# Expert tile rows turned by VectorE from four feature groups, gates spread by a block transpose

## What is computed

```
def _L0_ffn_ref(x, gate_w, gate_b, w1, b1, w2, b2, w3, b3):
    K = 2
    logits = jnp.einsum('bsd,de->bse', x, gate_w) + gate_b
    probs = jax.nn.softmax(logits, axis=1)
    vals, idx = jax.lax.top_k(probs, K)
    h = relu(einsum('bsd,edo->ebso', x, w1) + b1[:, None, None, :])
    h = relu(einsum('ebso,eop->ebsp', h, w2) + b2[:, None, None, :])
    y = relu(einsum('ebso,eop->ebsp', h, w3) + b3[:, None, None, :])
    onehot = one_hot(idx, E)
    w_tok = einsum('bske,bsk->bse', onehot, vals)
    v = einsum('ebso,bse->eo', y, w_tok)
    return einsum('bse,eo->bso', onehot.max(axis=2), v)
```

## Time and profile before

| | us |
|---|---|
| median of 3 runs (1003.84, 1006.84, 1004.35) | 1004.35 |
| span of the profiled execution | 1003.7 |
| expert stage in it, PE's first transpose to the end of the last unit | 437.9 to 669.6 |

### The profile page before, as it was taken

The page is one execution under the profiler, slowest core; times in us unless marked ns, Lnnn a source line. Parts: engine busy times, 40 slices in busy tenths (PEclk is TensorE's granted clock), DMA queues, the critical chain, the costliest instruction groups (busy, mean ns, idle before and its releaser), DMA issues. The chain is left out here.

```text
span 1003.7 us, 19227 instructions
## 1 busy us (share of the span) xinstructions
PE 934.0 (93%) x7747; PEld 757.2 (75%) x7747; DVE 429.3 (43%) x994; ACT 346.5 (35%) x886; POOL 250.9 (25%) x306
## 2 busy tenths in 40 slices
PE   5999999989998889999999999999889899999994
PEld 5977776676775644789999999987765578999532
DVE  2973454224442647002112132135267630656576
ACT  2322323245552124122222233324276611122374
POOL 5452111023554306000000010004065403000275
PEclk9999999999999979899999999997969998999996
DMA  9994000245622807259999888700040032971001
GB/s 254 382 331 127 2 2 2 98 152 203 238 120 95 309 7 254 55 181 386 358 383 313 284 269 283 254 29 28 4 153 3 2 119 78 321 247 66 1 15 51
DMA packets 72456, 162.01 MB, mean 161 GB/s; under 512 B 4132, under 2 KB 5685, under 8 KB 70321
## 3 DMA queue, kind: packets, MB, share of 16 engines
q1 hardware_dynamic: 70048, 156.54, 45.8%
q0 software_dynamic: 2320, 4.25, 1.4%
HBM read 128.81 MB, written 31.97 MB: 160 GB/s over the span
## 5 line engine op out<-in xcount | busy, mean ns | idle before, releaser
L2113 PE MATMUL ps<-ffn_h,ffn_w 128*128 128x128 f32 x1280 | 149.1, 275 | 0.0
L2113 PEld LDWEIGHTS ps<-ffn_h,ffn_w 128*128 128x128 f32 x1280 | 145.9, 192 | 0.0
L2113 PE MATMUL ps<-ffn_xh,ffn_w 128*128 128x128 f32 x640 | 74.9, 275 | 0.3 <-ACT ffn_xh L2147 0.3
L2203 DVE TENSOR_SCALAR ffn_h<-ps,tile_bias 128x128 f32<-128x128 f32 x80 | 22.5, 345 | 122.4 <-PE ps L2113 122.4
L2113 PEld LDWEIGHTS ps<-ffn_xh,ffn_w 128*128 128x128 f32 x640 | 73.1, 192 | 0.9 <-issue 0.9
L1418 POOL TENSOR_TENSOR ctx_low<-shelf,ctx_high 128x1024 fp32r<-128x1024 f32 (+2 forms) x24 | 43.0, 1819 | 65.4 <-PE ps L1283 33.7
L2161 ACT ACTIVATE ffn_y<-ffn_y 128x128 f32<-128x128 f32 x80 | 23.7, 298 | 73.9 <-DVE ffn_y L2219 73.9
L1526 PE MATMUL ps<-x_qT,ctx_ct 128*128 128x100 f32 (+1 forms) x384 | 46.4, 284 | 2.3 <-PEq L137 2.0
L1526 PEld LDWEIGHTS ps<-x_qT,ctx_ct 128*128 128x128 f32 (+1 forms) x384 | 45.0, 197 | 3.7 <-issue 3.2
L2219 DVE SCALAR_TENSOR_TENSOR ffn_y<-ps,tile_bias,ffn_gate_row 128x128 f32<-128x128 f32 x80 | 22.6, 344 | 58.0 <-PE ps L2113 57.9
L2834 POOL TENSOR_TENSOR att_e<-att_e,decay 100x400 f32<-100x400 f32 x32 | 32.7, 1033 | 46.1 <-DVE att_e L2685 46.1
(11 more groups left out here) (469 smaller groups left out, 2096.8 us busy)
## 6 DMA issues: line engine op xcount, KB each, us to landing
ffn_w<-in_L_ffn_w_dram SPq DMA_DIRECT2D x60, 1024.0 KB, 6.0
shelf<-in_ctx_dram SPq DMA_DIRECT2D x12, 1280.0 KB
expert_rows<-nothing SPq DMA_DIRECT2D x1, 14820.0 KB, 49.6
context_turned<-ctx_ct SPq DMA_DIRECT2D x8, 1444.0 KB, 7.9
ctx_ct<-context_turned SPq DMA_DIRECT2D x8, 1444.0 KB, 12.5
ctx_lent<-in_ctx_dram SPq DMA_DIRECT2D x4, 1280.0 KB
rows_own<-expert_rows SPq DMA_DIRECT2D x8, 260.0 KB, 3.0
x_wo<-in_L_xattn_Wo_dram SPq DMA_DIRECT2D x1, 2048.0 KB, 9.5
```

The lines of the kernel that those rows point to most:

```text
L2113: mm = nc.tensor.matmul(acc(n)[:, m, :], w[:, n % SLOTS, k, m * P:(m + 1) * P], into[l][:, i % 2, k, :], start=k == 0, stop=k == C - 1, sk ...
L2203: nc.vector.tensor_scalar(h2[:, i % 2, m, :], acc(n)[:, m, :], bsel[:, m, i, 1:2], 0.0, ALU.add, ALU.max).then_inc(h2_kept, 1)
```

## The change

**Loading the rows.** The one DMA of a tile becomes eight. For each block n of 32 rows, one DMA loads the 512 features as four groups of 128: the group f of the block's row r goes to partition 32 f + r, columns 128 n to 128 n + 127. A second DMA loads the 8 gates of these 32 rows onto each of the four groups of 32 partitions, into the new buffer `gates_raw`, with a semaphore of its own.

**Turning them.** DVE's transpose turns each 32x32 block in place of it. With the rows laid out in four groups, one such instruction of 128x512 gives `xh` directly: partition 32 f + d' of column (n, k, r) is feature 128 f + 32 k + d' of row 32 n + r. PE's transposes and ACT's copies are gone. A product k of the first layer now sums over the features 128 f + 32 k + d' instead of 128 k + p, so the first layer's weights must have their rows in that order: `load_unit` loads l = 0 as four DMAs of 256 KB, one for each k, whose source walks 4 groups x 32 rows x 2 KB. Its right-hand side is four pieces of 32 columns. The other two layers are loaded as before.

**Gates.** POOL and DVE work on four columns of gates at once; a second DVE transpose, of the broadcast 128x4 gates, puts them on all partitions. PE's product and ACT's copy are gone.

**Order.** The 14 later gathers stand behind every second unit load (odd n, 5 to 31) instead of behind each; the six `last` loads follow at n = 32 to 37.

The diff, cut to its core:

```diff
+        first_w = g["L0_ffn_w1"].rearrange("e (f k d) o -> f d e k o", f=HPC, k=C)
+        expert_w = [g[f"L0_ffn_w{i}"].rearrange("e (c p) o -> p e c o", p=P) for i in (2, 3)]
...
+            if l == 0:
+                for k in range(C):
+                    sp.dma_start(w[:, n % SLOTS, k, :], first_w[:, :, bass.ds(expert, 1), k, :].rearrange("f d a o -> f d (a o)")
+                                 ).then_inc(w_landed[n % SLOTS], 16)
+            else:
+                sp.dma_start(w[:, n % SLOTS, :, :], expert_w[l - 1][:, bass.ds(expert, 1)].rearrange("p a c o -> p (a c) o")
+                             ).then_inc(w_landed[n % SLOTS], 16)
...
-            sp.dma_start(rows_of_tile(i), rows_dram[bass.ds(row, P), :]).then_inc(gathered[i], 16)
+            here = rows_dram[bass.ds(row, P), :]
+            for n in range(HPC):
+                sp.dma_start(rows_of_tile(i)[:, n * P:(n + 1) * P],
+                             here[n * HD:(n + 1) * HD, 0:D].rearrange("r (f d) -> f r d", d=P)).then_inc(gathered[i], 16)
+                sp.dma_start(gates_raw[:, i, n, :],
+                             here[n * HD:(n + 1) * HD, D:XW].unsqueeze(0).to_broadcast([HPC, HD, E])).then_inc(gathered_gates[i], 16)
...
                     if n >= SLOTS - 1 and more < MT:
-                        gather(sp, more)
-                        more += 1
+                        if n % 2:
+                            gather(sp, more)
+                            more += 1
...
-                def turn(i):
-                    pe.wait_ge(gathered[i], 16)
...
-                def spread_gate(i):
-                    pe.wait_ge(gate_col, i + 1)
...
+                            rhs = xh[:, i % 2, :, k, :] if l == 0 else into[l][:, i % 2, k, :]
...
-                def keep(i):
-                    act.wait_ge(turned, i + 1)
...
+                def turn(i):
+
+                    dve.wait_ge(gathered[i], 16 * HPC)
+                    if i >= 2:
+                        unit_made(dve, i - 2, 0)
+                    nc.vector.transpose(xh[:, i % 2].rearrange("p i k r -> p (i k r)"), rows_of_tile(i)[:, 0:D]).then_inc(kept, 1)
...
+                def spread_gate(i):
+
+                    dve.wait_ge(gate_col, i + 1)
+                    if i >= 2:
+                        dve.wait_ge(weighed, C * (i - 1))
+                    nc.vector.transpose(gate_row[:, i % 2, :], gate[:, i % 2, :].unsqueeze(2).to_broadcast([P, HPC, HD])
+                                        ).then_inc(rows_kept, 1)
```

More of the change, by code:

```diff
@@ L1678, in program @@
         w_landed = [sem(f"ffn_landed{s}") for s in range(SLOTS)]
+        parts_of = lambda n: C if units[n][1] == 0 else 1
+        landed_by = [16 * sum(parts_of(m) for m in range(n % SLOTS, n + 1, SLOTS)) for n in range(len(units))]
         def expert_of(sp, i):
@@ L1777, in program @@
         fold_bank = lambda n: ps[:, (7, 0, 1)[n % 3], :]
-        gathered = [sem(f"rows_gathered{i}") for i in range(MT)]
+        gathered, gathered_gates = ([sem(f"{what}_gathered{i}") for i in range(MT)] for what in ("rows", "gates"))
         def gather(sp, i):
             row = sp.value_load(table[0:1, 1, i:i + 1], min_val=0, max_val=SPARE)
-            sp.dma_start(rows_of_tile(i), rows_dram[bass.ds(row, P), :]).then_inc(gathered[i], 16)
+            here = rows_dram[bass.ds(row, P), :]
[4 more added lines that the diff above has]
+                             here[n * HD:(n + 1) * HD, D:XW].unsqueeze(0).to_broadcast([HPC, HD, E])).then_inc(gathered_gates[i], 16)
         with nc.Block() as block:
@@ L2064, in _ @@
                 for s in range(SLOTS):
-                    sp.wait_ge(w_landed[s], 16 * (len(units) // SLOTS))
+                    sp.wait_ge(w_landed[s], landed_by[len(units) - SLOTS + s])
             @block.tensor
             def _(pe):
-                def turn(i):
-                    pe.wait_ge(gathered[i], 16)
-                    if i >= 2:
-                        pe.wait_ge(kept, i - 1)
-                    for c in range(C):
-                        mm = nc.tensor.transpose(ps[:, 3 + i % 2, c * P:(c + 1) * P], rows_of_tile(i)[:, c * P:(c + 1) * P],
-                                                 ident[:, :])
-                    mm.then_inc(turned, 1)
-                def spread_gate(i):
-                    pe.wait_ge(gate_col, i + 1)
-                    if i >= 2:
-                        pe.wait_ge(rows_kept, i - 1)
-                    else:
-                        pe.wait_ge(tile_kept, 2)
-                    nc.tensor.matmul(grow(i), gate[:, i % 2, :].to_broadcast([P, P]), ident[:, :],
-                                     start=True, stop=True).then_inc(gate_rows, 1)
                 def turn_sum(c):
@@ L2112, in layer @@
                                 pe.wait_ge((h1_kept, h2_kept)[l - 1], C * i + k + 1)
+                            rhs = xh[:, i % 2, :, k, :] if l == 0 else into[l][:, i % 2, k, :]
                             mm = nc.tensor.matmul(acc(n)[:, m, :], w[:, n % SLOTS, k, m * P:(m + 1) * P],
[L2114 removed]
+                                                  rhs, start=k == 0, stop=k == C - 1,
                                                   skip_group_check=True)
                     mm.then_inc(made, 1)
[L2118 removed]
                 for n, (i, l) in enumerate(units):
[L2120 to L2123 removed]
                     if n in SUM_AT:
@@ L2162, in total @@
                                              accum_out=vT[:, m, i:i + 1]).then_inc(counted, 1)
-                keep(0)
                 for n, (i, l) in enumerate(units):
-                    if n + 1 < len(units) and units[n + 1][1] == 0:
-                        keep(units[n + 1][0])
                     if 0 <= n - PREP_AT - 1 < len(PREP):
@@ L2209, in gate_of @@
                     if i >= 2:
-                        dve.wait_ge(gate_rows, i - 1)
-                    nc.vector.tensor_reduce(gate[:, i % 2, :], gates[:, i % 2, :], AX.X, ALU.add).then_inc(gate_col, 1)
+                        dve.wait_ge(rows_kept, i - 1)
+                    nc.vector.tensor_reduce(gate[:, i % 2, :], gates[:, i % 2], AX.X, ALU.add).then_inc(gate_col, 1)
+                def spread_gate(i):
[4 more added lines that the diff above has]
+                                        ).then_inc(rows_kept, 1)
                 def weigh(n, i):
@@ L2220, in weigh @@
                                                        ALU.add, ALU.mult).then_inc(weighed, 1)
+                turn(0)
                 for n, (i, l) in enumerate(units):
+                    if n + 1 < len(units) and units[n + 1][1] == 0:
+                        turn(units[n + 1][0])
                     if l == 0:
@@ L2225, in _ @@
                     elif l == 1:
+                        spread_gate(i)
                         second_layer(n, i)
```

34 lines of the change are left out of this document (9 added, 25 removed).

## The result

The changed kernel takes 1239.98 us (median, 1234.31 to 1241.47) beside 1003.84 us for the kernel before: 1.233 times as long (95% interval 1.230 to 1.236), 236 us more. The profiled execution took 1234.31 us, with a span of 1232.4; it is the shortest of the five runs, 5.7 us under their median.

A forecast was written before the change was run, and what follows sets the result against it. PE bound the kernel before; after the change four DMA engines would, with 422 us of queue, moving the last unit's end from 669.6 to 853: 1004.35 + 183 + 13 (clock) = 1200 us, range 1140 to 1350.

The forecast's parts named there:

- The mechanism: DMA queue: first-layer weights, rows and gates, read with outermost count 4 onto 128 partitions, use only four of 16 engines.
- The rival with 16 engines: Expert-stage DMAs: the SBUF side's 128 decides, so all 16 engines work; chance 0.16, of which 0.11 for 996 us.
- The packet: DMA engines: 2 KB on one engine takes 83.6 ns, from 24.5 GB/s an engine.
- The round, 16.05 us: Expert stage, each of the four engines: 10.7 us for a first-layer load plus two other loads at 2.68 us.
- The gather, 5.76 us: Row and gate loads on each of four engines: 3.2 us of 512 B pieces, 2.6 of 32 B; bounds 4.1 to 19.2.
- the rival of 65 to 125 ns for each: Gathers on four engines with slow 32 B pieces: 1315 us at 65 ns, about 1470 at 125; 0.04 for over 1350.
- That is on the path if nothing else is later: SP, routing block: 42 more gather issues, 16.8 us, end at 442, so the next block begins 5 us later.
- The sum: Four engines' queue from 419.5: gathers 115, first-layer loads 193, others 104, attention weights 10, together 422 us, ending at 842.
- Clock: PE in the expert stage: idling lowers its clock and costs 13 us, bounds 0 and 69.
- The hidden parts: DVE's two transposes a tile, 0.7 and 0.3 us, stay hidden, up to 2.9 us for the first.
- The rival's 996: Expert stage with 16 engines: 1004.35 less PE's 13 us plus SP's 5 gives 996 us; chance 0.11.
- What the profile should show: Expert stage: PE idle before first-layer units, DMA share not over 0.6, late loads, few SP waits, about 410 us.

The follow-up runs named there:

- the version with both edits: The changed kernel with first-layer weights and also rows and gates loaded by feature group (outermost count 32 instead of 4): 1063.02 us, ratio 1.057.
- 992 us, above: The changed kernel with natural-order weights in one DMA, three early gathers, features as whole rows in one DMA, gates by feature group: 992.39 us, ratio 0.988.

## Why the prediction was right, step by step, and where its sizes were off

**The mechanism.** "So a DMA takes the number of engines that divides its outermost count evenly" and "An even split of both sides is 4 engines" hold for a count of 4 onto 128 partitions: share 0.27 and 100 GB/s in the windows of after, and 177 us are back with an outermost count of 32. That "such DMAs share the same engines" holds as well: in the rounds without gathers the last four of the 16 events of the other loads are late, and rounds with gathers are longer than those without. The rival with 16 engines falls.

**The packet.** The 83.6 ns of "2 KB on one engine" are right where the four work alone: 100 GB/s, by which 1.05 MB would take 10.5 us.

**The round, 16.05 us.** It took 18.4, and this is the main term that was mis-sized. "Another load is 32 on each of 16, 2.68 us" held: the four spend 2.6 or 2.7 us on each. The step that failed is "A first-layer load is 512 such packets: 128 on each of four engines, 10.7 us". By the events it kept the four for 13.2, 13.0 and 13.6 us (827.2 to 840.4, 845.7 to 858.7, 864.0 to 877.6). The prediction priced it as if the four worked alone. For some 8 us of it the twelve move the next two loads, and in that stretch a 2 KB packet takes 129 ns in the mean (812 to 820), so that the four get 64 packets done and not 99; 35 packets of 84 ns are 2.9 us, by this estimate, where 2.5 are missing. Over 18 rounds it makes 18 x 2.4 = 43 us.

The number of engines alone does not make packets slow: 16 engines moved 387 GB/s in the kernel before, 89 ns a packet. Nor do the other loads, which are the same 1 MB onto 128 partitions. The end of the stage narrows it down. Behind the last first-layer load five of them stand in the queue. Until it lands (877.65, where PE begins its unit) the 16 engines move 270 GB/s, and right behind it 377 (the rows 873 to 877 and 877 to 881). So packets are slow on all 16 engines while the four move a first-layer load beside the others. In the kernel before with the four-engine load alone the rate goes from 285 GB/s (795 to 797) to 388 (799 to 801) as the last such load lands (798.3), and its round in this timeline is 722.70 - 703.35 = 19.35 us, so gathers and gates have no part in it:

```profile
703.35 5.47 PE L2121 MATMUL ps<-ffn_xh,ffn_w 128*128 128x128 f32 x32 [4.51 <-DMA ffn_w<-in_L_ffn_w_dram]
...
722.70 6.31 PE L2121 MATMUL ps<-ffn_xh,ffn_w 128*128 128x128 f32 x32 [6.08 <-DMA ffn_w<-in_L_ffn_w_dram]
```

Which property of the first-layer load slows the other engines down stays open; no version changed it alone.

**The gather, 5.76 us.** Eight rounds with 12 gathers took 711.49 - 502.33 = 209.2 us, 26.1 each, so a gather is (26.1 - 18.4) / 1.5 = 5.1 us. Over 20 gathers 13 us less than predicted. The 32 B pieces are cheap, as assumed (9 ns is the median of their packets from 419 to 461); the rival of 65 to 125 ns for each falls.

The Trainium skill ("DMA: Bandwidth & Descriptors", Specifications) has transfers under 512 B do a read-modify-write, by which the 32 B pieces would be nearer the high end. The 5.1 us of a gather leave, behind 3.2 us for the 512 B pieces, at most 1.9 us / 128 = 15 ns for one of 32 B, and no run shows such a penalty for this read.

**SP.** "One issue holds SP 0.35 us, with its register move some 0.4" was wrong: an issue with an outermost count of 4 holds it 0.55 us, 0.74 from one to the next, and the block ended 23.5 us later instead of 5. With 32 outermost, in the version with both edits, the same eight issues hold SP 0.32 to 0.38 us each, as the 0.35 of the earlier trace rows, so it is their form and not their number:

```profile
421.25 0.32 SPq L1796 DMA_DIRECT2D rows_own<-expert_rows  x1
421.75 0.32 SPq L1798 DMA_DIRECT2D ffn_gates_raw<-expert_rows  x1
...
422.67 0.38 SPq L1798 DMA_DIRECT2D ffn_gates_raw<-expert_rows  x1
```

"That is on the path if nothing else is later" was the safer half. The four engines were busy meanwhile, if not fully: the share is 0.18 from 419 to 461, where four in full work show 0.26 or 0.27. That is 42 x (1 - 0.18 / 0.265) = 13 us of queue lost. The version with three early gathers gets 7 to 10 of them back.

**The sum.** The last first-layer unit began at 877.65 where 830 was predicted: +43 for the rounds, -13 for the gathers, +13 for the start make +43 of these 48 us; 5 are not accounted for. That the gathers and the start cancel is luck.

**Clock.** "I take 13 us (bounds 0 and 69)": nearly nothing. PE ran at half clock in every round (805 to 807: 0.50), but the DMAs set the end. From 877.65 the last six units and the products between took 24.5 us instead of 22.5. So 2 us.

Together 853 + 13 us of clock was predicted for the end of the stage and 902 measured, 36 us later; behind it 4 us less were taken. The prediction also put the median 0.65 us over the span of the profile. It lies 7.6 us over it: the time of that execution is 1.9 us more than its span (1234.31, 1232.4), and the median 5.7 us more than that. 36 - 4 + 7 make 39 of the 40 us between 1200 and 1240.

**The hidden parts.** DVE's transposes take 0.70 and 0.31 us, as taken ("0.7 and 0.3"). The timeline of DVE has these rows for one tile:

```profile
618.01 0.70 DVE L2182 STREAM_TRANSPOSE ffn_xh<-xT_hi 128x512 f32<-128x512 f32 x1
...
623.93 0.31 DVE L2204 STREAM_TRANSPOSE ffn_gate_row<-ffn_gate 128x128 f32<-128x128 f32 x1
```

PE's 13.0 us are real and visible where DMA leaves them (992 us, above). The rival's 996 was missed even with 16 engines: the one form of the loads tried here that has both these 16 engines and the order that DVE's transpose needs writes into 32 partitions at a time, and it takes 1063. Whether another form does better was not tried.

**What the profile should show.** PE idle of several us ahead of each first-layer unit: 2.0 to 14.2 us, 143 in all for 18. A share "not over 0.6": 0.45 with gathers, 0.64 without, so a little over it. "A first-layer load landing tens of us after its issue": 28 us from the first of its four issues (812.29) to the last event (840.4). SP waiting for PE hardly at all: the list of SP's waits has no such line for the weights' DMAs, beside 54 waits before. "A stage of about 410 us": 441.

## What to carry to other kernels

Before a layout is changed so that another engine can do the work, read the outermost count of every DMA on both its sides, and compute the time of the engines that it leaves; a mean DMA share of half may be four engines that never rest. When such a load is cut to use all engines, cut it so that each DMA still covers all 128 partitions; here the cut of the weights' loads by partitions cost 32 to 43 us, and the cut by chunks nothing. And do not take the price of a packet for fixed: read alone or with 16 engines at work in the kernel before it was 84 to 89 ns, and beside the new loads it became 129. Here the price from before gave only a lower bound for the round.

## What was not expected of the hardware

- 16 engines writing into the same 32 partitions: 259 GB/s at a share of 1.07, beside 358 GB/s at 1.01 with the same packets on 128 partitions (the first is from a run of 1055.30 us). The same with 512 B row pieces: 285 GB/s at 1.09 beside 314 at 0.97.
- An issue of a DMA with an outermost count of 4 holds SP 0.55 us, beside 0.35 and 0.32 to 0.38 for the same eight issues with an outermost count of 32.
- While four engines move a first-layer load and the other twelve plain 1 MB loads, a 2 KB packet takes 129 ns on all of them (252 GB/s at a share of 0.99), beside 89 ns before (387 GB/s). When the last such load has landed the rate goes from 270 to 377 GB/s. The cause is open.
- The engines of one DMA do not wait for each other: the four loaded ones finish a plain load 7 to 8 us after the other twelve (816.4 and 824.6; 820.3 and 827.2).
